# A fused attention-and-expert block on one core: a new hand-searched order of all engines, and one bias addition moved from TensorE to VectorE

## The reference

```python
n = layernorm(x)                                   # over the last axis, eps 1e-5
q, k = rope(bf16(n @ Wq.T)), rope(bf16(n @ Wk.T))  # rotary position, base 32
scores = q @ k.T / sqrt(128)                       # causal, per batch of 2048 rows
o = where(causal, exp(scores), 0).sum(-1)          # one number per row
a = relu(o * fc1_w + fc1_b) @ fc2_w.T + fc2_b      # 16 inner values, 128 outputs
x = x + layernorm(a)
h = relu(layernorm(x) @ W1[1] + b1[1])             # 256 hidden values, one expert
x = x + layernorm(h @ W2[1] + b2[1])
```

## Time and profile before

| | us |
|---|---|
| runs | 92.93, 95.62, 94.38 |
| median | 94.38 |
| the profiled execution, its own time | 92.96 |
| its span, first to last instruction | 91.2 |
| granted TensorE clock, mean | 0.992 |

### The profile page before, as it was taken

The page is one execution under the profiler, slowest core; times in us unless marked ns, Lnnn a source line. Parts: engine busy times, 40 slices in busy tenths (PEclk is TensorE's granted clock), DMA queues, the critical chain, the costliest instruction groups (busy, mean ns, idle before and its releaser), DMA issues.

```text
span 91.2 us, 1530 instructions
## 1 busy us (share of the span) xinstructions
PE 82.5 (90%) x445; PEld 49.4 (54%) x445; DVE 78.5 (86%) x205; ACT 70.7 (78%) x201; POOL 59.2 (65%) x84
## 2 busy tenths in 40 slices
PE   4958999988899789998999999999999999999930
...
DVE  4469998999998999999998988998799689894961
ACT  5035899996998899999999999988669629545750
...
GB/s 39 268 252 298 285 267 227 208 88 0 115 7 115 7 115 4 0 0 115 0 0 0 7 0 0 0 0 0 115 0 90 36 4 53 62 0 163 67 235 110
DMA packets 11884, 7.64 MB, mean 84 GB/s; under 512 B 851, under 2 KB 10980, under 8 KB 11876
## 3 DMA queue, kind: packets, MB, share of 16 engines
...
## 4 chain that ended last, share of the span: by engine, by line
PE 59%; ACT 14%; DVE 9%; DMA 7%; issue 3%; SPq 2%; POOL 2%; POOLq 1%; DVEq 0%
PE psum L724 19%; PE psum L798 14%; ACT psum L553 11%; PE psum L750 11%; PE psum L716 6%; DMA x_s<-x 4%; PE psum L777 3%; DMA qk_swap<-qk 3%; DVE rows_n L348 2%; POOL rstd L489 2%; ACT fc L566 2%; DVE qk_r L383 2%; DVE qk_swap L383 2%; PE psum L769 1%; DVE qk L505 1%
## 5 line engine op out<-in xcount | busy, mean ns | idle before, releaser
L489 POOL TENSOR_TENSOR rstd<-ve,half_neg 128x4 f32<-128x4 f32 (+2 forms) x38 | 35.0, 930 | 23.1 <-DVE ve L354 18.7
L553 ACT ACTIVATE psum<-psum 128x1024 f32<-128x1024 f32 (+7 forms) x48 | 36.6, 763 | 1.2 <-PE psum L754 0.8
L750 PE MATMUL psum<-qk_r 128*128 128x512 bf16 (+3 forms) x80 | 19.7, 348 | 1.7 <-DVE qk_r L417 1.0
L798 PE MATMUL psum<-w_c,hid 128*128 128x128 f32 x128 | 16.0, 277 | 0.0
L798 PEld LDWEIGHTS psum<-w_c,hid 128*128 128x128 f32 x128 | 15.5, 192 | 0.8 <-issue 0.3
L724 PE MATMUL psum<-cols_n,wqk 128*128 128x512 f32 (+1 forms) x36 | 15.8, 553 | 0.0
L724 PE MATMUL psum<-cols_n,w_c 128*128 128x512 f32 (+1 forms) x36 | 15.7, 550 | 0.0
L750 PEld LDWEIGHTS psum<-qk_r 128*128 128x128 bf16 x80 | 6.7, 98 | 13.0 <-ACT psum L553 4.8
L716 PE MATMUL psum<-ident,rows_n 128*128 128x128 f32 x64 | 10.2, 277 | 0.9 <-DVE rows_n L348 0.9
L638 DVE BATCH_NORM_STATS2 stats<-psum 128x6 f32<-128x256 f32 x23 | 8.7, 419 | 1.5 <-PE psum L798 1.0
L664 DVE SCALAR_TENSOR_TENSOR x<-psum,rstd,x_s 128x128 f32<-128x128 f32 x32 | 9.1, 343 | 1.0 <-POOL rstd L489 0.9
...
## 6 DMA issues: line engine op xcount, KB each, us to landing
...
out<-x_s SPq DMA_DIRECT2D x4, 64.0 KB, 1.7
```

Of the source, the lines that this page charges most:

```text
L489: ready[k].done(eng.tensor_tensor(rstd[:, g, STAT_SLOT[k], t], ve[:, g, STAT_SLOT[k], t], half_neg[:, 0:tiles], ALU.pow), n)
L553: exps.done(eng.activation(area, area, ACT.Exp, scale=scale_qk, accum_out=sums[:, g, s, j:j + 1]), n, j, s)
L750: mm = eng.matmul(psum[:, own[0] + i, 0:width], query, qk_r[:, g0 + c, 1, 0:width], start=True, stop=c < gb)
L798: mm = eng.matmul(bank[:, j * P:(j + 1) * P], hid[:, g, h, (j0 + j) * P:(j0 + j + 1) * P], w2_c[:, h, :], start=not seeded and h == 0, sto ...
```

## The change

The table STEPS is replaced by another order. It has the same steps but for these: one more unit of y has a `bias` step (units 0, 2, 4, 5, 6 where it was 0, 1, 2, 3), so TensorE seeds six units and not seven, two of four tiles and four of one; and there is one more blank step, of 384 columns. Steps that several engines can do are given out anew: both stat3 of ScalarE go to VectorE, +w1 too; ScalarE takes four more of +h0 and +h1 and four fewer of +q and +tr1, and squares 16 tiles in stat5 where it was 12; both cos steps of GpSimd go to VectorE, and GpSimd takes rope of units 1 and 2. The banks are chosen anew. The code around the table is unchanged, and since the table is one line longer, its lines have numbers one higher. Two lines of the table:

```diff
-load_x.4 blank.8#7 blank.1.256#7 load_x.3 mask.0 load_wqk.0 load_x.1 load_x.0 repeat.0 stat1.4 load_fc.0 eps1.4.D
...
+load_x.3 blank.7#7 blank.1.256#7 load_wqk.0 repeat.0 load_x.0 mask.0 load_x.4 load_w2.0 load_x.8 stat1.3 load_b2.0
...
```

More of the change, by code:

```diff
@@ new lines @@
+norm1.6.P k.4#4 +q.4.D k.8#2 +k.4.A cos.3.D eps1.7.A swap.4 tr1.2#0 eps1.1.A sin.3.D +k.8.A q.8#4 rstd1.1 +tr1.2.A
+rope.3.D load_table.3 +k.0.A tr1.6#2 rstd1.7 norm1.1.D +q.8.A scores.2.3.0#3 cos.4.D +tr1.6.A scores.2.0.0#0
+scores.2.1.0#1 swap.8 tr1.1#4 cos.8.D exp.2.0.0 scores.2.2.0#5 k.6#2 exp.2.1.0 sin.4.D eps1.5.A exp.2.2.0 q.6#1
+rstd1.5 rope.4.D exp.2.3.0 +tr1.1.D +k.6.A scores.3.0.0#56 norm1.7.P +q.6.D scores.3.3.0#34 exp.3.0.0 q.1#2 swap.6
+sum.2.D exp.3.3.0 scores.3.2.0#01 cos.0.D sin.8.D scores.3.1.0#56 k.2#7 exp.3.2.0 rope.8.D tr1.7#3 cos.6.D exp.3.1.0
```

34 lines of the change are left out of this document (added).

## The result

The changed kernel is slower by 1.2%: median 94.36 us (20 runs) against 93.42 us for the kernel before, run beside it (20 runs), ratio 1.0119, 95% interval 1.0085 to 1.0153. The forecast was a ratio of 0.992. Every kernel has some longer executions: the ratios leave out those that lie more than 1.5% above the kernel's shortest, the medians are those of all. The profiled execution took 94.22 us (before 92.96) at a granted clock of 1.0, its span is 92.4 us (before 91.2).

What follows compares the result with a forecast made beforehand. TensorE bounds the kernel, paced by ScalarE until 41.33 us, then by its own work. Terms 17.9 + 0.3 + 37.3 + 0.1 + 29.2 + 0.95 = 85.75, plus 4.7, give span 90.4, execution 92.2, median 93.6 us; range 91.5 to 95.5.

Steps and rivals of the forecast that it cites:

- ScalarE before the first exponential: Front of the kernel: ScalarE has 11.0 us of work there, first exponential at 17.9 us, 18.5 if b2 lands late.
- Rival C: Front: b2 or w2 lands 1.5 us late, delaying q, k, swap and first exponential; median 95.5, chance 0.17.
- The sum for the start of the last y: First exponential to last y: 17.9 + 0.3 + 37.3 + 0.1 + 29.2 + 0.95 = 85.75 us, against 86.72 before.
- The margins of 0.6 us: Pairs from exp.6.0.0 on: ScalarE frees the bank about 0.6 us after TensorE's own work would reach it.
- the late shortfall: TensorE's late stretch: counted steps run short of the trace by 1.24 us, of which 0.95 is kept.
- the pacing term: From the first exponential to exp.6.3.1 near 55.5 us ScalarE holds TensorE: 37.3 us of work, 0.3 idle.
- The start: Front: VectorE normalises group 4 without waiting for the fourth load; transposes at 6.5 us instead of 7.09, gain 0.6.
- the walk: Step-by-step count of the front: rope.3 done at 16.0 us, not 17.0, and first exponential at 17.7.
- Rival A: Whole kernel, faster by over 2%: exponentials start at 17.2 us, ScalarE never idles; median 92.2, chance 0.25.
- Rival B: Late chain from fc2.4 to trz.4: TensorE waits 0.9 us and the gain is lost; median 94.5, chance 0.16.
- The tail: End, from last y: 4.7 us, 0.2 more than before, as out.4 stands directly ahead of GpSimd's four powers.
- The port: Port shared by VectorE and GpSimd, between 17 and 23 us: the new order gains VectorE 0.5 to 1.3 us.

Runs made afterwards that it cites:

- f2: Changed kernel with b2's transfer reading 128 different rows of w2, not one row 128 times, bytes and order equal: ratio 0.9921 to the kernel before, median 92.42 us.

## Why the prediction was wrong, and where it was right

The step that failed is the term "ScalarE before the first exponential", 17.9 us, and in it the price of b2's load. I took it near the end at which b2 causes no wait "because 4.6 us was measured behind 2.1 MB of loads and there will be 1.2 MB" (by the list of transfers the first figure is 1.97 MB). It took 5.8 us, and x of unit 2 with it landed at 10.46 us. The reasoning by bytes ahead in the queue was the error: with equal bytes and an equal queue, and another source, b2 takes 3.7 us (f2) and is there when ScalarE wants it. Rival C had the path: q, k, swap and the first exponential move together, and no cover is left later because ScalarE paces TensorE. Its condition, a first exponential later than 18.7 us, is met with 19.42, and b2 lands 1.51 us after it is wanted, as C had it. Not in C is that the loads of x come late with it, and the chain runs through one of them and not through the wait for b2. What the wait for b2 would cost alone was not tried. C's figure was 95.5 on a median of 94.38, a ratio of 1.012, and that is what was measured, with some luck: ScalarE idles 0.3 us and not 0.9, and the part behind is longer by about as much.

- The sum for the start of the last y was 85.75, the trace has 87.79: 2.04 more. Of these 1.52 are the first exponential (19.42 against 17.9). 0.5 are the part behind: I had ScalarE's last hold at exp.6.3.1 after 0.3 of idle time and 37.3 us of work, and it is in front of fc2 of unit 0 after 27.0 us, the idle 0.3 included, with 41.3 us of TensorE behind it where the counted steps give 39.9. So 27.0 + 0.1 + 41.3 = 68.4 stands for my 0.3 + 37.3 + 0.1 + 29.2 + 0.95 = 67.85. The margins of 0.6 us, at which I saw TensorE held in each later pair, were smaller than the error of the counting. The mis-sized term is the late shortfall: 1.35 us behind the hold, not 0.95 behind a hold some ten us later. This is the second step that failed, and one of my signs said so: TensorE free of ScalarE well before 50 us, here at 46.5, means that the pacing term is wrong. It cost 0.5 us.
- The start was right: transposes at 6.5, measured 6.57. Swap issue 11.0 and rope.3 done at 16.0 are wrong for the changed kernel (12.88 and 18.03) and right for f2 (10.99 and 16.11). Its first exponential of 17.56 lies by the 17.7 of the walk.
- The forecast of the ratio, 0.992, is that of f2, 0.9921. So the gain that I read from the order is there, of the size forecast, and the loss of 2.0% comes on top of it. That the figures agree so closely is in part luck: f2's first exponential is 0.34 us earlier than 17.9, and its part behind is 0.4 us longer than mine.
- Rival A is out: ScalarE does idle 0.3 us only, as it asked, but even f2's first exponential is not at 17.2. Rival B is out: in the changed kernel's chain the stretch from 46.54 us on is TensorE without a wait, trz.4 included.
- The tail was right: 4.7 forecast, 4.6 measured, with out.4 directly ahead of the small powers.
- The port: the term of 0.5 to 1.3 us for VectorE was right at its upper end. VectorE's four norms of 512 columns on x_s have a mean of 686 ns (before 888), its cos products of 1024 columns 684 ns (before 762, six of them), together 4 x 0.20 + 6 x 0.08 = 1.3 us less. What that gives in the total was not tried. A norm on GpSimd at 14.68 us takes its short 1.04 us, where the earlier trace rows had 1.55, and the rope sum of unit 3 0.69:

```profile
14.68 1.04 POOL L349 TENSOR_TENSOR rows_n<-x_s,rstd 128x512 f32<-128x512 f32 x1
```

```profile
17.34 0.69 DVE L418 TENSOR_TENSOR qk_r<-qk_r,qk_swap 128x1024 bf16<-128x1024 bf16 x1
```
